# Softmax attention: maxima taken two banks at a time, from four, and no bank kept for transposes

## The chip, the cores and the metric

The kernel runs on one core of one Trainium2 chip. The metric is the device time of the whole program in microseconds (us). Three runs of the kernel before gave 2098.14 to 2100.54 us, median 2099.5.

## The reference

Two transformer-like blocks, each `x = x + attention(layernorm(x)) * silu(ffn(layernorm(x)))`, on `x` of 2 x 2048 x 128 in float32. The first block has linear attention and a top-2 mixture of 8 experts. The second has softmax attention and a top-1 mixture of 8 experts. The change touches only the softmax attention of the second block, cut here to what matters:

```python
b, s, _ = x.shape                       # 2, 2048
q, k, v = (x @ w.T).reshape(b, s, 16, 8)      # 16 heads of 8
q, k = rope(rms_norm(q)), rope(rms_norm(k))
scores = einsum('bqhd,bkhd->bhqk', q / sqrt(8), k)
attn = softmax(scores, axis=-1)         # over 2048 keys
out = einsum('bhqk,bkhd->bqhd', attn, v).reshape(b, s, 128) @ wo.T
```

## The kernel before, in words

The program has stages that follow one another. The first block and the routing, experts and operand preparation of the second fill the first third of the time. Then `softmax_attention` (L1375 to L1692) runs, and `finish` ends the program.

**Chunks.** `softmax_attention` treats two heads of one batch entry at a time (a pair; 16 pairs) and 512 queries at a time (a chunk; 4 per pair, 64 in all). The two heads lie in the two halves of the partitions, 64 rows each. Every chunk has two parts.

**The maxima.** For each block of 128 queries, head and 512 keys, TensorE makes a 128 x 512 tile of scores, queries on the partitions (`for_maxima`, L1507: 32 per chunk), into one of three PSUM banks, in turn. VectorE reduces each to its row maximum (`maxima`, L1659: 32 per chunk), and then all of them to the negated maximum of each query and head (`negate`, L1667). GpSimd splits that into three bf16 parts (`parts`, L1455 to L1465), TensorE transposes them (`shifts`, L1517) into half of bank 7, and ScalarE copies them into rows of the query operand (`take_shifts`, L1623, two copies), so that the next product of keys and queries comes out with the maximum already subtracted.

**The weights.** TensorE makes the scores again, keys on the partitions (`score`, L1524: 32 of 128 x 512 per chunk, three banks in turn). ScalarE takes the exponential (L1630). TensorE multiplies the values by it (`weigh`, L1538: 16 calls per chunk, each four matmuls in the four column tiles of 32, recorded as 8) and accumulates into bank 6; the column tiles are four consecutive `s`, so key tile parity and head, and the two halves of the 512 queries lie in the two halves of the bank. The 33rd value column is ones, so the sum of the exponentials comes out too. At the end of a chunk ScalarE copies the bank (L1648), TensorE transposes the copy and adds the parities (`transposed_sums`, L1582: four matmuls, recorded as 8) into the other half of bank 7, and VectorE takes the reciprocal (L1685) and multiplies (L1690).

**Order.** Each engine's order is written out by hand, and nothing is rearranged at run time. TensorE's main loop makes, at each step `s` of chunk `n`, `score(n, s)` and one maximum of a later chunk: at `s = 8` that is maximum 24 of chunk `n + 1`, so at `s = 16` it goes over to chunk `n + 2`. At every even `s` a `weigh` follows the maximum. After `s = 27` come the shifts of the next chunk, after the last step the transposed sums. A score waits until the exponential has left its bank (three steps earlier); a maximum waits until VectorE has left its bank (three maxima earlier):

```python
pe.wait_ge(m_out, m.at(S, a - earlier(a) + 1 + M_FREE))     # for_maxima
pe.wait_ge(p_ready, n.at(S, s - earlier(s) + 1 + P_FREE))   # score
```

ScalarE's order is the exponentials, with the two shift copies after the 28th and the copy of the sums after the fourth of the next chunk. VectorE's order is the maxima, the negation, and, before maximum 24 of a chunk and after it, the reciprocal and the product of an earlier chunk.

Next to this run SP's loads of the query and key operands of a pair (two pairs ahead) and, during the last two pairs, GpSimd's gathers of the experts' rows.

Of the kernel before, what the change touches and what calls it, by code (L numbers as in the profile page):

```python
# [11 lines left out]
P = 128  # L12
# [40 lines left out]
class Step:  # L53


    def __init__(self, turn, per_turn, number):
        self.turn, self.per_turn, self.number = turn, per_turn, number

    def __add__(self, n):
        return Step(self.turn, self.per_turn, self.number + n)  # L60

    def at(self, each, more):

        constant = self.number * each + more
        return constant if self.turn is None else self.turn * (self.per_turn * each) + constant


# [29 lines left out]
def constants(k, pool):  # L97
# [12 lines left out]
    pool.memset(k.sum_parity[:, :], 0.0).then_inc(cleared, 1)  # L110
# [13 lines left out]
    for group in range(4):  # L124
        head = group % 2
        cols = k.sum_parity[:, 9 * head:9 * head + 9]
# [1238 lines left out]
def softmax_attention(k, U, V, attn, gather):  # L1365
# [7 lines left out]
    UNROLL = 2  # L1373
    S = 2 * NK
    R = 3  # L1375
    PR = 16
    S_BANK, M_BANK, O_BANK, T_BANK = 0, 3, 6, 7
    AHEAD = 24
    SHIFTS_AFTER = 6
    EARLY = 4  # L1380
    NPAIRS = BATCH * PAIRS
    with ExitStack() as ctx:
# [4 lines left out]
        tops = sb("tops", [P, 2, 2 * TPC, QC])  # L1387
# [3 lines left out]
        sumsT = sb("sumsT", [P, CHUNK])  # L1391
        inv = sb("inv", [P, 2 * TPC])
        (cleared, copy_allowed, v_loaded, m_ready, m_out, neg_ready, shift_step, shift_ready, shiftT_ready,
         shift_in, s_ready, p_ready, p_used, sums_out, turned, inv_ready, attn_out) = (
            sem(n) for n in ("cleared", "copy_allowed", "v_loaded", "m_ready", "m_out", "neg_ready",
                             "shift_step", "shift_ready", "shiftT_ready", "shift_in", "s_ready", "p_ready", "p_used",
                             "sums_out", "turned", "inv_ready", "attn_out"))
        q_loaded, k_loaded = k.q_loaded, k.k_loaded
        block = ctx.enter_context(nc.Block())
        GATHERED = TILES // (UNROLL * QC)  # L1400

        M_FREE, P_FREE, U_FREE, O_FREE, T_FREE = R, R, PR // 4, 1, 1
        G = 4

        ahead = Core()
        ahead.turn = None

        def two_on(n):

            return Step(ahead.turn, n.per_turn, n.number + 2 - (0 if n.turn is None else n.per_turn))  # L1410

        def turns(eng, body):
            for pair in range(NPAIRS):
                ahead.turn = None
                body(Step(None, 0, pair), Step(None, 0, pair * QC), pair % 2, pair == NPAIRS - 1)

        @block.sync
        def _(sp):
            for pair in range(2, NPAIRS):

                sp.wait_ge(p_used, (pair - 1) * QC * S // G + U_FREE)
                load_rows(k, sp, U, pair, 0, q_loaded[pair % 2])
                load_rows(k, sp, U, pair, 1, k_loaded[pair % 2])

        @block.gpsimd
        def _(pool):
            pool.memset(shift[:, :, :], 0.0).then_inc(cleared, 1)

            pool.sem_inc(m_out, M_FREE)
            pool.sem_inc(p_ready, P_FREE)  # L1430
            pool.sem_inc(p_used, U_FREE)
            pool.sem_inc(sums_out, O_FREE)
            pool.sem_inc(attn_out, T_FREE)

            def before_copy():

                pool.sem_inc(copy_allowed, 1)

            def load(pair, par):

                before_copy()
                for h in range(2):
                    src = V[:, :, bass.ds(pair.at(2 * DK, h * DK), DK)]
                    nc.gpsimd.tensor_copy(values[par][:, :, h, 0:DK], src).then_inc(v_loaded, 1)

            def parts(m):

                pool.wait_ge(neg_ready, m.at(1, 1))
                if m.turn is not None or m.number > 0:
                    pool.wait_ge(shiftT_ready, m.at(1, 0))  # L1450
                place = lambda i: shift[:, :, :].rearrange("p t (h r) -> p h t r", h=2)[:, :, :, SHIFT + i]
# [3 lines left out]
                nc.gpsimd.tensor_copy(place(0), src).then_inc(shift_step, 1)  # L1455
                pool.wait_ge(shift_step, m.at(4, 1))
                nc.gpsimd.tensor_tensor(rest[0], src, place(0), ALU.subtract).then_inc(shift_step, 1)
                pool.wait_ge(shift_step, m.at(4, 2))
                before_copy()
                nc.gpsimd.tensor_copy(place(1), rest[0]).then_inc(shift_step, 1)  # L1460
                pool.wait_ge(shift_step, m.at(4, 3))
                nc.gpsimd.tensor_tensor(rest[1], rest[0], place(1), ALU.subtract).then_inc(shift_step, 1)
                pool.wait_ge(shift_step, m.at(4, 4))
                before_copy()
                nc.gpsimd.tensor_copy(place(2), rest[1]).then_inc(shift_ready, 1)  # L1465

            pool.wait_ge(cleared, 1)
            for h in range(2):
                nc.gpsimd.tensor_copy(values[0][:, :, h, 0:DK], V[:, :, h * DK:(h + 1) * DK]).then_inc(v_loaded, 1)
            parts(Step(None, 0, 0))  # L1470

            def pair_steps(pair, chunk, par, final):
                for c in range(QC):
                    if not (final and c == QC - 1):
                        parts(chunk + (c + 1))
                    if c == 0 and not final:

                        pool.wait_ge(p_used, pair.at(QC * S // G, U_FREE))
                        load(pair + 1, 1 - par)
                    if pair.number >= NPAIRS - UNROLL:  # L1480
                        first = ((pair.number - (NPAIRS - UNROLL)) * QC + c) * GATHERED
                        for t in range(first, first + GATHERED):
                            gather(pool, t)

            turns(pool, pair_steps)

        half_of = lambda s: s % 2
        other_half_of = lambda a: 1 - a % 2  # L1490
        head_rows = lambda h: slice(h * HEAD_ROWS, (h + 1) * HEAD_ROWS)

        def earlier(s):

            return next(d for d in range(1, 2 * R + 1) if (s - d) % S % R == s % R and (s >= d or (s - d + S) % R == s % R))

        @block.tensor
        def _(pe):
            pe.wait_ge(cleared, 1)

            def for_maxima(m, c, par, a):

                h, qt, kb = other_half_of(a), a // 2 // QC, a // 2 % QC
                rows = head_rows(h)
                pe.wait_ge(m_out, m.at(S, a - earlier(a) + 1 + M_FREE))
                at = (c * TPC + qt) * P
                nc.tensor.matmul(bank[:, M_BANK + a % R, :], queries[par][rows, at:at + P],  # L1507
                                 keys[par][rows, kb * CHUNK:(kb + 1) * CHUNK], start=True, stop=True).then_inc(m_ready, 1)

            def shifts(m):  # L1510

                pe.wait_ge(shift_ready, m.at(1, 1))
                if m.turn is not None or m.number > 1:
                    pe.wait_ge(attn_out, m.at(1, T_FREE - 1))
                out = bank[:, T_BANK, :].bitcast(BF16)
# [4 lines left out]
            def score(n, c, par, s):  # L1520

                pe.wait_ge(p_ready, n.at(S, s - earlier(s) + 1 + P_FREE))
                rows = head_rows(half_of(s))
                nc.tensor.matmul(bank[:, S_BANK + s % R, :], keys[par][rows, (s // 2) * P:(s // 2 + 1) * P],  # L1524
                                 queries[par][rows, c * CHUNK:(c + 1) * CHUNK], start=True, stop=True).then_inc(s_ready, 1)

            def weigh(n, par, g, half):

                if g == 0 and half == 0:
                    pe.wait_ge(sums_out, n.at(1, O_FREE))
                pe.wait_ge(p_ready, n.at(S, 4 * g + 4 + P_FREE))
                at = slice(half * (CHUNK // 2), (half + 1) * (CHUNK // 2))
                for j in range(G):
                    s = G * g + j
                    mm = nc.tensor.matmul(bank[32 * j:32 * j + 32, O_BANK, at], values[par][:, s // 2, s % 2, :],  # L1538
                                          probs[:, s % PR, at], start=(g == 0 and half == 0), stop=(g == S // G - 1 and half == 1),
# [4 lines left out]

            zero = Step(None, 0, 0)
            pe.wait_ge(q_loaded[0], 16 * LOADS[0])
            pe.wait_ge(k_loaded[0], 16 * LOADS[1])
            for a in range(S):
                for_maxima(zero, 0, 0, a)
            for a in range(AHEAD):  # L1550
                for_maxima(zero + 1, 1, 0, a)
                if a == AHEAD // 2:
                    shifts(zero)
            pe.wait_ge(shift_in, 2)
            for s in range(2 * G):
                score(zero, 0, 0, s)
# [399 lines left out]
```

## Time and profile before

| | |
|---|---|
| median of three runs | 2099.5 us (2098.14 to 2100.54) |
| the profiled execution | 2101.37 us, its span 2099.6 us |
| granted TensorE clock, mean of the span | 0.924 of full speed |
| softmax attention | from about 672 us to 2079 us of the span |
| from the first negation of the maxima to the last | 692.1 to 2048.5 us, 63 chunks |

The table's times are those of one execution that was profiled; all durations below come from it. Its own time is 1.9 us above the median of the runs. A start is counted from the beginning of the span. PE is TensorE's matmul, PEld its load of stationary operands, DVE is VectorE, ACT is ScalarE, POOL is GpSimd, SP is SyncE.

### The profile page before, as it was taken

What the parts mean: (1) busy time and instruction counts of PE and PEld (TensorE: products, weight loads), DVE (VectorE), ACT (ScalarE), POOL (GpSimd) and SP (SyncE); (2) the same over time, 40 slices, a digit from 0 to 9 for tenths busy, and PEclk for the clock granted to TensorE, in tenths of its full rate; (3) what the DMA queues carried; (4) which work ended last, traced back from release to release, by engine and by line L of the source; (5) the groups of instructions that cost most, each with busy time, mean ns of one, the idle gap of its engine ahead of it and who ended that gap; (6) DMA issues with size and microseconds to landing.
All of it is one profiled execution on the core that took longest, in us unless ns stands there. A gap on an engine that the chain in (4) does not pass through costs nothing. (4 is left out here: it accounts for less than half of the span.)

```text
span 2099.6 us, 42125 instructions
## 1 busy us (share of the span) xinstructions
PE 1758.9 (84%) x16301; PEld 749.7 (36%) x16301; DVE 1631.6 (78%) x2868; ACT 1462.6 (70%) x2761; POOL 336.0 (16%) x620
## 2 busy tenths in 40 slices
PE   5865879507855999999999999999999999999998
PEld 4544743406832232323333333333333333323334
DVE  3742437624367899999999999999999999999992
ACT  2103546203443588888888888888888888888988
POOL 2371027353032000000000000000000000001211
PEclk9887998558976699999999999999999999999999
DMA  7014111312102001001010010110100101001001
GB/s 243 21 53 114 46 48 52 93 35 70 32 1 32 1 2 17 10 9 17 2 17 14 4 17 2 16 17 1 17 6 13 17 1 17 10 8 22 16 12 51
DMA packets 64253, 61.73 MB, mean 29 GB/s; under 512 B 10720, under 2 KB 52704, under 8 KB 64064
## 3 DMA queue, kind: packets, MB, share of 16 engines
q1 hardware_dynamic: 57920, 46.56, 9.7%
q0 software_dynamic: 6144, 12.60, 2.0%
q8 instruction: 125, 2.05, 0.4%
q14 instruction: 64, 0.52, 0.1%
HBM read 23.21 MB, written 22.94 MB: 22 GB/s over the span
## 5 line engine op out<-in xcount | busy, mean ns | idle before, releaser
L1659 DVE TENSOR_REDUCE at_tops<-bank 128x1 f32<-128x512 f32 x2048 | 1264.1, 683 | 62.4 <-PE bank L1507 43.0
L1630 ACT ACTIVATE at_probs<-bank 128x512 f32<-128x512 f32 x2048 | 1109.6, 598 | 141.3 <-PE bank L1524 114.5
L1507 PE MATMUL bank<-keys,queries 64*128 64x512 bf16 x2048 | 682.0, 390 | 20.8 <-DVE at_tops L1659 19.1
L1524 PE MATMUL bank<-queries,keys 64*128 64x512 bf16 x2048 | 650.5, 383 | 56.2 <-ACT at_probs L1630 56.2
L1538 PE MATMUL bank<-at_probs,values 128*32 128x256 f32 x8192 | 655.5, 392 | 12.2 <-ACT at_sumsT L1648 8.7
L1524 PEld LDWEIGHTS bank<-queries,keys 64*128 64x128 bf16 x2048 | 131.1, 93 | 510.3 <-ACT at_probs L1630 362.8
L1538 PEld LDWEIGHTS bank<-at_probs,values 128*32 128x32 f32 x8192 | 161.8, 108 | 326.8 <-ACT at_probs L1630 191.0
L1455 POOL CAST at_shift<-at_neg 128x8 bf16<-128x8 f32 x64 | 14.0, 219 | 1239.7 <-DVE at_neg L1667 1239.7
L1507 PEld LDWEIGHTS bank<-keys,queries 64*128 64x128 bf16 x2048 | 169.8, 93 | 113.6 <-DVE at_tops L1659 85.2
L669 DVE COPY ep_weights<-WB 128x642 f32 x72 | 35.8, 497 | 91.4 <-DVE ep_slots L680 46.6
L1623 ACT ACTIVATE queries<-bank 3x512 bf16<-3x512 bf16 x128 | 75.4, 589 | 31.4 <-PE bank L1517 28.3
L1096 DVE COPY ffn_w<-W 128x512 f32 x39 | 19.9, 511 | 83.7 <-issue 42.4
L696 ACT ACTIVATE ep_hT<-bank,ep_weights 128x128 f32<-128x128 f32 x144 | 45.1, 365 | 48.8 <-PE bank L638 48.7
L1195 PE MATMUL bank<-wqkv,xnT 128*128 128x384 f32 x64 | 40.0, 801 | 37.6 <-DVE op_qk L1317 32.5
L303 POOL DMA_INDIRECT sorted_pairs<-g_rows,pair_slot x64 | 62.4, 974 | 52.0 <-DVE pair_slot L550 32.8
L1582 PE MATMUL bank<-sum_parity,at_sumsT 128*128 128x18 f32 x512 | 68.2, 267 | 0.8 <-ACT at_sumsT L1648 0.8
L638 PE MATMUL bank<-ep_slotsT,ep_weights 128*128 128x128 f32 x288 | 52.0, 305 | 19.3 <-DVE ep_weights L669 19.3
L1582 PEld LDWEIGHTS bank<-sum_parity,at_sumsT 128*128 128x128 f32 x512 | 61.9, 191 | 15.5 <-issue 15.5
L733 POOL DMA_INDIRECT g_rows<-made_of_pairs,pair_slot x32 | 31.2, 975 | 142.1 <-SPq L714 132.6
L830 DVE RECIPROCAL qg_den<-qg_den 128x512 f32<-128x512 f32 x8 | 26.8, 3353 | 34.0 <-ACT qg_den L799 34.0
L1103 ACT ACTIVATE ffn_slotsT<-bank 128x512 f32<-128x512 f32 (+1 forms) x10 | 5.7, 586 | 67.1 <-PE bank L1039 66.8
L638 PEld LDWEIGHTS bank<-ep_slotsT,ep_weights 128*128 128x128 f32 x288 | 38.7, 196 | 31.2 <-DVE ep_weights L669 29.6
(248 smaller groups left out, 1522.5 us busy)
## 6 DMA issues: line engine op xcount, KB each, us to landing
queries<-query_parts SPq DMA_DIRECT2D x192, 32.0 KB
keys<-key_parts SPq DMA_DIRECT2D x192, 32.0 KB
sorted_pairs<-zeros SPq DMA_DIRECT2D x16, 288.0 KB, 3.7
ep_slots<-sorted_pairs SPq DMA_DIRECT2D x6, 768.0 KB, 9.2
made_of_pairs<-ep_slots SPq DMA_DIRECT2D x6, 768.0 KB, 4.1
sorted_tokens<-zeros SPq DMA_DIRECT2D x8, 312.0 KB, 3.4
ffn_slots<-sorted_tokens SPq DMA_DIRECT2D x3, 832.0 KB, 7.7
made_of_sorted<-ffn_slots SPq DMA_DIRECT2D x3, 832.0 KB, 4.3
```

The source lines that it names most:

```text
L303: pool.indirect_dma_start(sorted_dram, bass.IndirectOffsetOnAxis(ap=r0.slot[i][:, t:t + 1], axis=0), rows[:, t, :], None).then_inc(scatter ...
L638: mm = nc.tensor.matmul(bank[:, H_BANK + u, i * P:(i + 1) * P], wt[:, u, i * P:(i + 1) * P], slotsT[:, j // TPC % TR, j % TPC * P:(j % TPC ...
L669: nc.vector.tensor_copy(wt[:, j % R, :], WB[:, bass.ds(at, STRIDE0)]).then_inc(w_ready, 1)
L696: nc.scalar.activation(hT[:, u, i * P:(i + 1) * P], bank[:, H_BANK + u, i * P:(i + 1) * P], ACT.Relu, bias=wt[:, u, B1_AT + i:B1_AT + i + ...
L1195: mm = nc.tensor.matmul(bank[:, t, 0:3 * D], xnT[:, at:at + P], w.wqkv[:, :], start=True, stop=True)
L1507: nc.tensor.matmul(bank[:, M_BANK + a % R, :], queries[par][rows, at:at + P], keys[par][rows, kb * CHUNK:(kb + 1) * CHUNK], start=True, st ...
L1524: nc.tensor.matmul(bank[:, S_BANK + s % R, :], keys[par][rows, (s // 2) * P:(s // 2 + 1) * P], queries[par][rows, c * CHUNK:(c + 1) * CHUN ...
L1538: mm = nc.tensor.matmul(bank[32 * j:32 * j + 32, O_BANK, at], values[par][:, s // 2, s % 2, :], probs[:, s % PR, at], start=(g == 0 and ha ...
L1582: mm = nc.tensor.matmul(bank[:, T_BANK, 256 + 18 * t:256 + 18 * (t + 1)], sumsT[:, t * P:(t + 1) * P], k.sum_parity[:, :], start=True, sto ...
L1623: nc.scalar.activation(queries[par][rows, c * CHUNK:(c + 1) * CHUNK], bank[rows, T_BANK, 0:CHUNK // 2].bitcast(BF16), ACT.Copy).then_inc(s ...
L1630: nc.scalar.activation(probs[:, s % PR, :], bank[:, S_BANK + s % R, :], ACT.Exp).then_inc(p_ready, 1)
L1659: nc.vector.tensor_reduce(tops[:, m.number % 2, other_half_of(a) * TPC + a // 2 // QC, a // 2 % QC:a // 2 % QC + 1], bank[:, M_BANK + a % ...
```

## The change

Only `softmax_attention` and one constant change.

1. **Two banks per maximum.** The maxima have four banks (3 to 6), as two places of two banks. A unit is two tiles of one head and query block, 1024 keys. VectorE reduces both banks in one instruction of 128 x 1024: 16 per chunk in place of 32. TensorE's first tile of a unit waits until VectorE has left the whole place, two turns earlier (`turn_taken`).
2. **Transposes take turns.** The transposed sums have no bank of their own any more: they take one turn of the maxima's places per chunk (`sums_turn`), after the last unit of a chunk, and VectorE's reciprocal and product, now one behind the other after the negation, end that turn. The shifts take one turn of the scores' three banks, between `s = 27` and `s = 28` (`SHIFT_BANK`), so that score 30 waits for the two shift copies. Scores 28 and 29, and also 31 and 0 to 2 of the next chunk, wait for the exponential two steps earlier in place of three.
3. **Column tiles.** The four column tiles of `weigh` are query halves by heads of one key tile. The accumulator is 256 columns wide in place of 512, the copy of the sums too, and the transposed sums are two matmuls (recorded as 4) against 36 columns in place of four against 18. The order of heads among the scores and maxima changes: two steps of one head, then two of the other, a score and its neighbouring maximum always of different heads.
4. **Order.** The transposed sums of chunk `n - 1` come at `s = 15` of chunk `n`. The first `weigh` of a chunk moves from `s = 6` to `s = 8`, where there are then two in a row. The copy of the sums stands after the fourth exponential as before. The first eight scores are interleaved with the first maxima. The step of the main loop is otherwise the same: score, maximum, and at even `s` a `weigh`; `AHEAD = 24` stays.

Cut to its core (the pool's and SP's code changes in how it is written only; the constant `sum_parity` of 18 columns becomes `sum_columns` of 36):

```diff
+    UNITS = 2 * TPC * 2
+    HALF = CHUNK // 2
+    S_BANK, M_BANK, O_BANK = 0, 3, 7
+    SHIFTS_AT = 28
+    COPY_AT, SUMS_AT = 4, 16
+        head_of = lambda s: s // 2 % 2
+        unit_of = lambda u: (1 - u % 2, u // 4, u // 2 % 2)
+        score_bank = lambda s: S_BANK + (s if s < SHIFTS_AT else s + 1) % R
+        SHIFT_BANK = S_BANK + SHIFTS_AT % R
+        unit_turn = lambda m, u: m * UNITS + u + max(0, m - 2)
+        sums_turn = lambda n: min(n + 3, NCHUNKS) * UNITS + n
+        place = lambda turn: M_BANK + turn % 2 * 2
...
+            def maximum(m, a):
+                u = a // 2
+                h, qt, half = unit_of(u)
+                turn = unit_turn(m, u)
+                if a % 2 == 0 and turn >= 2:
+                    pe.wait_ge(turn_taken, turn - 1)
...
+                mm = nc.tensor.matmul(bank[:, place(turn) + a % 2, :], queries[pair % 2][rows, at:at + P],
+                                      keys[pair % 2][rows, kb * CHUNK:(kb + 1) * CHUNK], start=True, stop=True)
+                if a % 2:
+                    mm.then_inc(m_ready, 1)
...
+            def score(n, s):
+                if s == SHIFTS_AT + R - 1 and n + 1 < NCHUNKS:
+                    pe.wait_ge(shift_in, 2 * (n + 2))
+                else:
+                    before = s - R if s < SHIFTS_AT else s - R + 1
+                    if s < R:
+                        before += 1
+                    if n * S + before >= 0:
+                        pe.wait_ge(p_ready, n * S + before + 1)
...
+            def transposed_sums(n):
+                turn = sums_turn(n)
+                pe.wait_ge(turn_taken, turn - 1)
+                pe.wait_ge(sums_out, n + 1)
...
+            for n in range(NCHUNKS):
+                ahead = (n + 1) * S + AHEAD
+                for s in range(FIRST_SCORES, S if last else S + FIRST_SCORES):
+                    m = n + s // S
+                    score(m, s % S)
+                    if ahead < NCHUNKS * S:
+                        maximum(*divmod(ahead, S))
+                        ahead += 1
+                    if s == SHIFTS_AT - 1 and not last:
+                        shifts(n + 1)
+                    if s == SUMS_AT - 1 and n:
+                        transposed_sums(n - 1)
+                    if s % G in (0, 2):
+                        half = 0 if s % G == 2 else 1
+                        g = s // G - 1 - half
+                        m, g = n + g // (S // G), g % (S // G)
+                        if g or half:
+                            if g == 0:
+                                weigh(m, 0, 0)
+                            weigh(m, g, half)
...
+            def maxima(m):
+                for u in range(UNITS):
+                    h, qt, half = unit_of(u)
+                    at = place(unit_turn(m, u))
+                    dve.wait_ge(m_ready, m * UNITS + u + 1)
+                    nc.vector.tensor_reduce(tops[:, m % 2, h * TPC + qt, half:half + 1], bank[:, at:at + 2, :].rearrange("p b n -> p (b n)"),
+                                            X_AXIS, ALU.max).then_inc(turn_taken, 1)
...
+            for m in range(NCHUNKS):
+                maxima(m)
+                negate(m)
+                if m >= 2:
+                    sums(m - 2)
```

## Rows read from the trace of the kernel before

**Rows 1.** Page, busy time of each engine, its share, instructions

```profile
PE 1758.9 (84%) x16301; PEld 749.7 (36%) x16301; DVE 1631.6 (78%) x2868; ACT 1462.6 (70%) x2761; POOL 336.0 (16%) x620
```

**Rows 2.** Stretches: us, busy us (instructions) by engine, clock, DMA share, GB/s

```profile
672.00:700.00 28.00, 26.67 (x51) 4.80 (x51) 27.16 (x46) 0.53 (x1) 1.72 (x8) 0.50 0.00 1
717.57:2048.50 1330.93, 1246.53 (x12661) 408.46 (x12657) 1252.89 (x2171) 1180.59 (x2172) 95.93 (x364) 1.00 0.07 11
```

**Rows 3.** Groups by line, 717.57 to 2048.50: busy us, mean ns | idle before

```profile
L1659 DVE TENSOR_REDUCE at_tops<-bank 128x1 f32<-128x512 f32 x1984 | 1225.3, 683 | 55.2 <-PE bank L1507 35.8 <-issue 0.4
L1630 ACT ACTIVATE at_probs<-bank 128x512 f32<-128x512 f32 x1986 | 1078.0, 597 | 133.6 <-PE bank L1524 106.9
L1648 ACT ACTIVATE at_sumsT<-bank 128x512 f32<-128x512 f32 x62 | 37.0, 597 | 13.7 <-PE bank L1538 13.7
```

**Rows 4.** Timeline, TensorE, one chunk: start us, us, instruction

```profile
1404.76 0.39 PE L1524 MATMUL bank<-queries,keys 64*128 64x512 bf16 x1
1404.76 0.60 PE L1507 MATMUL bank<-keys,queries 64*128 64x512 bf16 x2
1404.99 0.38 PE L1524 MATMUL bank<-queries,keys 64*128 64x512 bf16 x1
1405.30 0.64 PE L1538 MATMUL bank<-at_probs,values 128*32 128x256 f32 x8
1405.87 0.39 PE L1524 MATMUL bank<-queries,keys 64*128 64x512 bf16 x1
...
1409.55 0.39 PE L1507 MATMUL bank<-keys,queries 64*128 64x512 bf16 x1
1409.87 0.64 PE L1538 MATMUL bank<-at_probs,values 128*32 128x256 f32 x8
1410.44 0.39 PE L1524 MATMUL bank<-queries,keys 64*128 64x512 bf16 x1
...
1410.76 0.40 PE L1517 MATMUL bank<-identb,at_shift 128*128 128x128 bf16 x4
1411.09 0.39 PE L1524 MATMUL bank<-queries,keys 64*128 64x512 bf16 x1
```

**Rows 5.** Timeline, VectorE, the same chunk

```profile
1404.52 0.19 DVE L1667 TENSOR_REDUCE at_neg<-at_tops 128x8 f32<-128x32 f32 x1
1408.82 0.68 DVE L1659 TENSOR_REDUCE at_tops<-bank 128x1 f32<-128x512 f32 x1
1415.78 0.69 DVE L1659 TENSOR_REDUCE at_tops<-bank 128x1 f32<-128x512 f32 x1 [0.21 <-PE bank L1507]
...
1421.28 0.21 DVE L1690 TENSOR_TENSOR xnT<-bank,at_inv 128x64 f32<-128x64 f32 x1
1421.56 4.28 DVE L1659 TENSOR_REDUCE at_tops<-bank 128x1 f32<-128x512 f32 x7
```

**Rows 6.** Timeline, the matmul just before a reduction that waited

```profile
1415.33 0.60 PE L1507 MATMUL bank<-keys,queries 64*128 64x512 bf16 x2
```

**Rows 7.** Groups by line, VectorE, whole span, operands of 1024 elements

```profile
L1317 DVE TENSOR_TENSOR op_qk<-bank,op_st 128x1024 f32<-128x1024 f32 x8 | 9.8, 1224 | 0.3
L1305 DVE TENSOR_REDUCE op_st<-op_squares 128x128 f32<-128x1024 f32 x8 | 9.7, 1218 | 27.8 <-ACT op_squares L1233 27.8
```

**Rows 8.** Timeline, ScalarE, around the shift copies of that chunk

```profile
1405.18 0.60 ACT L1630 ACTIVATE at_probs<-bank 128x512 f32<-128x512 f32 x1 [0.68 <-PE bank L1524]
1405.68 0.59 ACT L1630 ACTIVATE at_probs<-bank 128x512 f32<-128x512 f32 x1
1410.16 1.30 ACT L1630 ACTIVATE at_probs<-bank 128x512 f32<-128x512 f32 x2
1411.48 1.20 ACT L1623 ACTIVATE queries<-bank 3x512 bf16<-3x512 bf16 x2
1412.71 2.73 ACT L1630 ACTIVATE at_probs<-bank 128x512 f32<-128x512 f32 x5
```

**Rows 9.** Timeline, TensorE and VectorE, transposed sums; last the end of the stage

```profile
1418.90 0.39 PE L1507 MATMUL bank<-keys,queries 64*128 64x512 bf16 x1
1419.21 1.07 PE L1582 MATMUL bank<-sum_parity,at_sumsT 128*128 128x18 f32 x8
1420.21 0.39 PE L1524 MATMUL bank<-queries,keys 64*128 64x512 bf16 x1
1420.32 0.21 DVE L1685 RECIPROCAL at_inv<-bank 128x8 f32<-128x8 f32 x1 [0.26 <-PE bank L1582]
2062.59 0.21 DVE L1685 RECIPROCAL at_inv<-bank 128x8 f32<-128x8 f32 x1 [13.91 <-PE bank L1582]
2062.83 0.22 DVE L1690 TENSOR_TENSOR xnT<-bank,at_inv 128x64 f32<-128x64 f32 x1
2074.48 1.83 PE L1538 MATMUL bank<-at_probs,values 128*32 128x256 f32 x24
```

**Rows 10.** Groups by line, ScalarE, a copy of 256 columns from PSUM

```profile
L413 ACT ACTIVATE kr_kvT<-bank 128x256 f32<-128x256 f32 x2 | 0.8, 384 | 17.4 <-PE bank L354 17.4
```

**Rows 11.** Waits, 717.57 to 2048.50: us in total, times, longest us

```profile
PEld bank L1524 <- ACT at_probs L1630: 349.3, 807, 0.7
PEld bank L1507 <- DVE at_tops L1659: 58.0, 173, 0.8
DVE at_tops L1659 <- PE bank L1507: 35.8, 124, 0.4
```

More of the change, by code:

```diff
@@ L50 @@
     pass
[L53 to L65, printed above, removed]
 def bc(ap, shape):
@@ L1470, in _ @@
[L1470 to L1495, printed above, removed]
+            load(0)
+            parts(0)
+            for n in range(NCHUNKS):
+                pair, c = divmod(n, QC)
+                if n + 1 < NCHUNKS:
+                    parts(n + 1)
+                if c == 0 and pair + 1 < NPAIRS:
+                    if pair:
+                        pool.wait_ge(p_used, n * S // G)
+                    load(pair + 1)
+                if pair >= NPAIRS - 2:
+                    first = (n - (NPAIRS - 2) * QC) * GATHERED
+                    for t in range(first, first + GATHERED):
+                        gather(pool, t)
@@ L1518, in shifts @@
                 mm.then_inc(shiftT_ready, 1)
[L1520 to L1527, printed above, removed]
-                if g == 0 and half == 0:
[L1533 to L1539, printed above, removed]
+            def score(n, s):
+                pair, c = divmod(n, QC)
+                if s == SHIFTS_AT + R - 1 and n + 1 < NCHUNKS:
+                    pe.wait_ge(shift_in, 2 * (n + 2))
+                else:
+                    before = s - R if s < SHIFTS_AT else s - R + 1
+                    if n == 0 and s == 0:
+                        pe.wait_ge(shift_in, 2)
+                    if s < R:
+                        before += 1
+                    if n * S + before >= 0:
+                        pe.wait_ge(p_ready, n * S + before + 1)
+                rows = head_rows(head_of(s))
+                at = keys_of(s) * P
+                nc.tensor.matmul(bank[:, score_bank(s), :], keys[pair % 2][rows, at:at + P],
+                                 queries[pair % 2][rows, c * CHUNK:(c + 1) * CHUNK], start=True, stop=True).then_inc(s_ready, 1)
@@ new lines, in weigh @@
+            def weigh(n, g, half):
+                pair, c = divmod(n, QC)
+                if g == 0 and half == 0:
+                    if c == 0:
+                        pe.wait_ge(v_loaded, 2 * (pair + 1))
+                    if n:
+                        pe.wait_ge(sums_out, n)
+                pe.wait_ge(p_ready, n * S + G * g + 3 + half)
+                kt = 2 * g + half
+                for j in range(4):
+                    q, h = divmod(j, 2)
+                    s = G * g + 2 * h + half
+                    mm = nc.tensor.matmul(bank[32 * j:32 * j + 32, O_BANK, 0:HALF], values[pair % 2][:, kt, h, :],
+                                          probs[:, s % PR, q * HALF:(q + 1) * HALF], start=(kt == 0), stop=(kt == NK - 1),
@@ L1615, in _ @@
-            turns(pe, pair_steps)
+                    shifts(0)
+                if a >= AHEAD - FIRST_SCORES:
+                    score(0, a - (AHEAD - FIRST_SCORES))
+            for n in range(NCHUNKS):
+                last = n == NCHUNKS - 1
+                ahead = (n + 1) * S + AHEAD
[17 more added lines that the diff above has]
+                            weigh(m, g, half)
@@ L1652, in _ @@
+            take_shifts(0)
+            for n in range(NCHUNKS):
+                for s in range(S):
+                    exponential(n, s)
+                    if s == COPY_AT - 1 and n:
+                        sums(n - 1)
+                    if s == SHIFTS_AT - 1 and n + 1 < NCHUNKS:
+                        take_shifts(n + 1)
+            sums(n)
         @block.vector
         def _(dve):
-            TAKEN = AHEAD
-            def maxima(m, of):
-                for a in of:
-                    dve.wait_ge(m_ready, m.at(S, a + 1))
-                    nc.vector.tensor_reduce(tops[:, m.number % 2, other_half_of(a) * TPC + a // 2 // QC, a // 2 % QC:a // 2 % QC + 1], bank[:, M_BANK + a % R, :], X_AXIS,
-                                            ALU.max).then_inc(m_out, 1)
```

257 lines of the change are left out of this document (86 added, 171 removed).

## Prediction

> **What bounds the kernel now.** I read the page first: over the whole span no engine is full [rows 1], but that is an average over stages. The stretch between the second and the last negation of the maxima is 62 equal chunks of softmax attention, 1330.93 / 62 = 21.47 us each, at TensorE's full granted clock, the higher of its two levels, 2.4 GHz [rows 2]. There VectorE is busy 94% of the time, TensorE 94% (modelled) and ScalarE 89%. Of VectorE's 20.2 us per chunk, 19.8 are the 32 maxima (1225.3 / 62), and it waits 0.9 us per chunk (55.2 / 62) just before one of them [rows 3]. Seven maxima in a row take 4.28 us [rows 5]: one each (4.28 - 0.68) / 6 = 0.60 us, though each lasts 0.68 until its end is known. So VectorE sets the pace now. The waits say the same: TensorE waits 58.0 us for VectorE to free a bank, in 173 places, VectorE only 35.8 for TensorE [rows 11].
>
> TensorE is close behind. Two steps (two scores, two maxima, one `weigh`) take 1405.87 - 1404.76 = 1.11 us: a score and its maximum run side by side, the next two start 0.23 later, the `weigh` 0.31 after them, and 0.57 after its start comes the next score [rows 4]. Sixteen of these are 17.8 us.
>
> **The two-bank reduction.** No reduction of two banks is in the trace. The nearest rows are a VectorE instruction that reads 1024 elements from two banks, 1.224 us, and a reduction of 1024 elements from SBUF, 1.218 us [rows 7]. Upper bound: two single ones, 2 x 0.68 = 1.36. I take 1.22. Since it is 0.54 longer than a single one, the next can start 0.60 + 0.54 - 0.01 = 1.13 us after it. Against 2 x 0.60 that saves 0.07 per unit, or 1.1 us per chunk, for an engine that is always fed.
>
> **The wait that comes with it.** Will it be fed? There are two places, so the maximum that opens a unit (M0) must wait until the reduction two turns earlier has ended. TensorE keeps its order: at 1409.55 a maximum had waited for the reduction that ran from 1408.82 to 1409.50, and the `weigh` behind it started only at 1409.87, the next score at 1410.44 [rows 4, 5]. In the new order M0 of every unit stands at an even `s`, and the `weigh` is right behind it; the unit's second maximum (M1) comes with the next score. The way round one place is therefore:
> - M0 to the score after the `weigh`, and M1 beside it: 1410.44 - 1409.55 = 0.89 [rows 4];
> - M1 to the start of its reduction: 1415.78 - 1415.33 = 0.45 [rows 5, 6];
> - the reduction until its end: 1.22 [rows 7];
> - end of a reduction to the maximum that waited for it: 1409.55 - 1409.50, 0.06 [rows 4, 5].
>
> That is 2.62 us per place, and with two places one unit every 1.31 us. This is longer than VectorE's 1.13, longer than TensorE's 1.11 and longer than 2 x 0.60 = 1.20 now. Before, three single banks gave 0.68 + 0.06 + 0.45 = 1.19 us of way against 3 x 0.60 = 1.80 of time: 0.6 to spare for a `weigh`. Now there is nothing to spare: the gap from M0 to M1 may be at most 2 x 1.13 - 0.45 - 1.22 - 0.06 = 0.53, and it is 0.89. VectorE will stand still 0.18 us before each unit, and TensorE 0.2 before each M0, with `weigh`, score and M1 queued behind. Sixteen units: 8 x 2.62 = 20.96 us.
>
> **The 17th turn.** The transposed sums take a turn. The next chunk's first unit uses the place of the last unit and follows it at 2.62 as ever; the second one takes the place of the sums, may follow the first at TensorE's pace, and its reduction 1.13 after the first's. VectorE's share (the negation 0.19, from reciprocal to product 2062.83 - 2062.59 = 0.24, from product to the next maximum 1421.56 - 1421.28 = 0.28 [rows 5, 9]) lies inside the way that TensorE needs. So from last unit to last unit: 2.62 + 1.13 + 7 x 2.62 = 22.09 us. The sums' own matmuls are halved (8 took 1.0 us up to the next score [rows 9], 4 about 0.5) and are ready before VectorE comes to them.
>
> **The shifts in the scores' banks.** I follow unit 5 (`s` = 26, 27) with M0 at 0. Score 27 at 0.89, its exponential 0.42 later at 1.31 (1405.18 - 1404.76 [rows 4, 8]). The shifts start 0.32 after score 27, score 28 0.33 later, at 1.54 [rows 4], a little late for its place. The copies start 0.62 after exponential 27 (the second of the two from 1410.16 starts at 1410.86, the copies at 1411.48) and take 1.20 [rows 8]: they end at 3.13. Score 29 at 2.43. Score 30, which could go at 2.65, now waits for the copies: 3.19, and M0 of unit 7 with it, 0.57 behind its place's time. The next exponentials start at 3.15 and 3.65 (they follow at 0.50: 1405.18, 1405.68 [rows 8]); score 31 waits for the second to end at 4.25, in place of 4.08. M1 of unit 7 is at 4.31, its reduction at 4.76 against 2.62 + 0.89 + 0.45 = 3.96: 0.80 us per chunk, on the place that hands over to the next chunk.
>
> **Two `weigh` in a row.** At `s` = 8 the gap from M0 to M1 grows by the second one. Its price isn't in the trace alone: three with their waits took 1.83 against 0.64 for one, so at most 0.60 each [rows 4, 9]; at least nothing. I take 0.5, as it has the passes of the first. The other place then comes 0.89 + 0.5 + 0.22 = 1.6 after it, not 1.2 to 1.3: 0.4 us. The free step at `s` = 6 returns almost nothing, since VectorE's 1.13 holds there.
>
> **The sum.** 22.09 + 0.80 + 0.40 = 23.3 us per chunk, 1.83 more than 21.47. Over 61 of the 62 chunks: +112 us. At the start TensorE runs at half clock with maxima alone (0.50 [rows 2]); 28 units there save 28 x 0.07 = 2 us, and the eight scores moved among them about 1: -3, with -6 to +1 as bounds. The last two chunks have no maxima and stay as they are. 2101.4 (the profiled execution's own time) + 109 = 2210; it stands 1.9 over the median, so **2208 us** is forecast.
>
> **Edits at no cost.** The copy of the sums goes from 0.597 [rows 3] to about 0.384 [rows 10]: ScalarE, 11% idle, gains 0.2 us that nobody waits for. The column tiles of `weigh` keep their number, size and passes. The wider constant is made long before. SP waits for the same count of `weigh` groups, and its loads run two pairs ahead with longer pairs to hide in; GpSimd's parts have 12 steps between the negation and the shifts. If TensorE became the bound, the halved sums would show as -0.5 per chunk.
>
> **A rule weighed against the trace.** VectorE's row in this stage is 94% busy, yet what ends its waits is TensorE [rows 2, 11]. The Trainium skill (Perfetto Trace Analysis, Optimizing Scalar/DVE Operations) has a rule for either case: grouping into larger operations helps where the engine is saturated; where it is not and leaves bubbles on other engines, breaking instructions up lets work be completed sooner. By its first half the time would be that of rival 1, by its second the one I forecast; the trace so far agrees with the first half for three single banks, and no row shows two places.
>
> **Rivals.**
> 1. *VectorE stays fed, and the change is faster* (0.09). If the `weigh` did not stand in the way round a place (gap of M0 to M1 under 0.53), a unit costs 1.13 and a chunk 16 x 1.13 + 0.8 = 18.9; with TensorE's 17.8 + 0.4 + 0.5 beside it, say 19.2: 2099.5 - 61 x 2.27 - 3 = 1958. For it: VectorE's share. Against it: rows that show `weigh` held behind a waiting maximum.
> 2. *Only the way round counts* (0.12): the stops at the shifts and the double `weigh` vanish in slack that I have missed. 22.09 per chunk: 2099.5 + 61 x 0.62 - 3 = 2134.
> 3. *Two banks cost as two instructions* (0.06): the change does not do what it says for VectorE. 1.36 gives (0.89 + 0.45 + 1.36 + 0.06) / 2 = 1.38 a unit, 1.2 more per chunk: 2208 + 61 x 1.2 = 2281. The rows of 1024 speak against it.
>
> My own case has 0.72; in 0.01 gains and stops cancel. Its own range is 2170 to 2245: the reduction between 1.20 and 1.30, the second `weigh` between 0 and 0.6, the stops at the shifts 0.4 less or 0.2 more, the start's bounds. The range of 8 in 10 takes in rival 2: 2130 to 2245. A difference of 0.2%, 4 us, is about what can be told from none: slower 0.90, same 0.01, faster 0.09.
>
> **What would show it.** Right: negations 23.3 us apart; reductions of about 1.22 us that start 1.1 to 1.5 apart, 1.31 on average; idle time of VectorE before most of them, ended by the maxima's matmul, near 0.2 each; a long wait of PEld at the maxima for VectorE in hundreds of places; score 30 of each chunk waiting for the shift copies; VectorE's busy share down from 94% to about 85%. Wrong: if reductions follow one another at 1.13 with no idle time, my way round a place is wrong; if they last 1.36, rival 3; if TensorE's clock in the stage falls from 1.00, every gap on it grows and the time passes 2245.

## The result, and the profile after

The changed kernel takes 2208.4 us (median of four runs, 2206.5 to 2210.3), the kernel before 2100.0 in the same comparison: a ratio of 1.0513, 95% interval 1.0498 to 1.0529. It is slower by 5%; 2208 was forecast. One of the four runs of the single-bank kernel with two repairs (below) took 5250.6 us and the other three 1999.4 to 2001.6, so its median and its ratio are of those three.

The whole difference lies in the softmax stage. From the second negation of the maxima to the last there are again 62 chunks, now in 1441.86 us: 23.26 each against 21.47 [rows 2]. That is 1441.86 - 1330.93 = 110.9 us more. From the first negation to the second it takes 21.3 us in place of 25.5, from the start of the span to the first it takes 2.3 us more, and from the last negation to the end it takes 51.1 us in both kernels. 110.9 - 4.2 + 2.3 = 109.0, which is the difference of the two spans, 2208.6 - 2099.6.

First the page of the kernel after, then the stretch of the 62 chunks and the groups by line in it, as in [rows 1 to 3]:

```profile
PE 1856.8 (84%) x16045; PEld 753.3 (34%) x16045; DVE 1589.5 (72%) x1844; ACT 1448.9 (66%) x2761; POOL 336.3 (15%) x620
```

```profile
715.65:2157.51 1441.86, 1348.38 (x12399) 412.70 (x12396) 1211.44 (x1176) 1166.37 (x2170) 95.89 (x364) 1.00 0.06 10
```

```profile
L1623 DVE TENSOR_REDUCE at_tops<-bank 128x1 f32<-128x1024 f32 x992 | 1180.3, 1221 | 221.7 <-PE bank L1484 220.3
L1598 ACT ACTIVATE at_probs<-bank 128x512 f32<-128x512 f32 x1984 | 1076.3, 598 | 242.0 <-PE bank L1513 229.3
...
L1604 ACT ACTIVATE at_sumsT<-bank 128x256 f32<-128x256 f32 x62 | 23.8, 384 | 30.7 <-PE bank L1529 30.7
```

VectorE does less: 992 reductions of 1.221 us in place of 1984 of 0.683 [rows 3], 1211 us busy in place of 1253 [rows 2]. But it is now busy 84% of the stretch, not 94%, because it stands 221.7 us before the maxima in place of 55.2. ScalarE does the same exponentials and stands 242 us before them in place of 134. No engine is full; TensorE's granted clock is 1.00, its higher level, as before. The waits of the same stretch say who holds whom (the scores, then both directions between VectorE and the maxima, last score 30 behind the shift copies; compare [rows 11]):

```profile
PEld bank L1513 <- ACT at_probs L1598: 450.7, 1037, 0.6
...
DVE at_tops L1623 <- PE bank L1484: 220.3, 557, 0.8
PEld bank L1484 <- DVE at_tops L1623: 156.0, 357, 0.5
PEld bank L1513 <- ACT queries L1590: 40.9, 62, 0.7
```

VectorE waits for TensorE 220 us (35.8 before) and TensorE for VectorE 156 us (58.0 before). Two engines that wait for each other, both with room, point to a way round that is too long. The timeline shows that way, first VectorE, then TensorE:

```profile
1414.00 1.23 DVE L1623 TENSOR_REDUCE at_tops<-bank 128x1 f32<-128x1024 f32 x1 [0.83 <-PE bank L1484]
...
1416.62 1.22 DVE L1623 TENSOR_REDUCE at_tops<-bank 128x1 f32<-128x1024 f32 x1 [0.27 <-PE bank L1484]
```

```profile
1415.28 0.39 PE L1484 MATMUL bank<-keys,queries 64*128 64x512 bf16 x1
1415.60 0.64 PE L1529 MATMUL bank<-at_probs,values 128*32 128x256 f32 x8
1416.17 0.39 PE L1513 MATMUL bank<-queries,keys 64*128 64x512 bf16 x1
1416.17 0.39 PE L1484 MATMUL bank<-keys,queries 64*128 64x512 bf16 x1
```

The reduction from 1414.00 ends at 1415.23; the first maximum of the next unit in its place starts 0.05 later; the `weigh` follows it, and only then, 0.89 after it, the second maximum; the reduction starts 0.45 after that, at 1416.62. From reduction to reduction in one place it takes 2.62 us.

### The profile page after: what moved, and what is told of

Read it like the earlier page. It is cut to its first block and busy times, and to the rows that moved or that the text cites. A ratio compares the mean times of both kernels' runs of the same rounds, so it can differ in the third digit from the quotient of the medians.

```text
span 2208.6 us, 40579 instructions
## 1 busy us (share of the span) xinstructions
PE 1856.8 (84%) x16045; PEld 753.3 (34%) x16045; DVE 1589.5 (72%) x1844; ACT 1448.9 (66%) x2761; POOL 336.3 (15%) x620
## 3 DMA queue, kind: packets, MB, share of 16 engines
HBM read 23.21 MB, written 22.94 MB: 21 GB/s over the span
## 5 line engine op out<-in xcount | busy, mean ns | idle before, releaser
L1623 DVE TENSOR_REDUCE at_tops<-bank 128x1 f32<-128x1024 f32 x1024 | 1217.9, 1221 | 225.9 <-PE bank L1484 224.6
L1484 PE MATMUL bank<-keys,queries 64*128 64x512 bf16 x2048 | 744.2, 392 | 23.0 <-DVE at_tops L1623 16.4
L1513 PE MATMUL bank<-queries,keys 64*128 64x512 bf16 x2048 | 672.8, 384 | 65.5 <-ACT at_probs L1598 28.4
L1529 PE MATMUL bank<-at_probs,values 128*32 128x256 f32 x8192 | 641.1, 390 | 0.0
L1513 PEld LDWEIGHTS bank<-queries,keys 64*128 64x128 bf16 x2048 | 144.4, 93 | 554.3 <-ACT at_probs L1598 462.2
L1484 PEld LDWEIGHTS bank<-keys,queries 64*128 64x128 bf16 x2048 | 177.9, 93 | 230.6 <-DVE at_tops L1623 185.1
L1529 PEld LDWEIGHTS bank<-at_probs,values 128*32 128x32 f32 x8192 | 168.0, 108 | 253.4 <-issue 241.1
L653 DVE COPY ep_weights<-WB 128x642 f32 x72 | 35.8, 497 | 88.6 <-DVE ep_slots L664 46.6
L622 PE MATMUL bank<-ep_slotsT,ep_weights 128*128 128x128 f32 x288 | 51.8, 304 | 19.2 <-DVE ep_weights L653 19.2
L1541 PE MATMUL bank<-sum_columns,at_sumsT 128*128 128x36 f32 x256 | 40.6, 284 | 14.0 <-DVE at_tops L1623 13.4
L1023 PE MATMUL bank<-ident,ffn_slots 128*128 128x128 f32 x39 | 8.3, 374 | 48.4 <-DMA ffn_slots<-sorted_tokens 48.1
```

The costliest lines, as they stand in the source:

```text
L622: mm = nc.tensor.matmul(bank[:, H_BANK + u, i * P:(i + 1) * P], wt[:, u, i * P:(i + 1) * P], slotsT[:, j // TPC % TR, j % TPC * P:(j % TPC ...
L653: nc.vector.tensor_copy(wt[:, j % R, :], WB[:, bass.ds(at, STRIDE0)]).then_inc(w_ready, 1)
L1484: mm = nc.tensor.matmul(bank[:, place(turn) + a % 2, :], queries[pair % 2][rows, at:at + P], keys[pair % 2][rows, kb * CHUNK:(kb + 1) * CH ...
L1513: nc.tensor.matmul(bank[:, score_bank(s), :], keys[pair % 2][rows, at:at + P], queries[pair % 2][rows, c * CHUNK:(c + 1) * CHUNK], start=T ...
L1529: mm = nc.tensor.matmul(bank[32 * j:32 * j + 32, O_BANK, 0:HALF], values[pair % 2][:, kt, h, :], probs[:, s % PR, q * HALF:(q + 1) * HALF] ...
L1541: mm = nc.tensor.matmul(out[:, :, t, :], sumsT[:, n % 2, t * P:(t + 1) * P], k.sum_columns[:, :].rearrange("p (q e) -> p q e", q=2), start ...
```

## The experiments

All times are medians; ratios are to the kernel before in the same comparison. "Per chunk" is the mean time between two negations of the maxima in the profiled execution, first interval left out. Unless said otherwise, an experiment changes the kernel after.

| | median us | ratio (95% interval) | per chunk us |
|---|---|---|---|
| the change | 2208.4 | 1.0513 (1.0498 to 1.0529) | 23.26 |
| weigh at odd steps | 2086.0 | 0.9923 (0.9907 to 0.9940) | 21.24 |
| scores three steps back | 2179.3 | 1.0366 (1.0349 to 1.0384) | 22.79 |
| no two weigh in a row | 2188.4 | 1.0410 (1.0393 to 1.0428) | 22.94 |
| single banks, four of them | 2046.5 | 0.9731 (0.9715 to 0.9748) | 20.65 |
| two banks, the three repairs | 2036.7 | 0.9702 (0.9686 to 0.9718) | 20.49 |
| the same, maxima before score 30 | 2036.8 | 0.9704 (0.9687 to 0.9720) | 20.49 |
| single banks, two repairs | 1999.7 | 0.9528 (0.9509 to 0.9547) | 19.93 |
| the same, maxima before score 30 | 1995.8 | 0.9503 (0.9487 to 0.9518) | 19.85 |
| two banks, later copy of the sums | 2002.1 | 0.9534 (0.9518 to 0.9550) | 19.93 |
| the same, maxima before score 30 | 2001.4 | 0.9533 (0.9517 to 0.9549) | 19.93 |
| the same, transposed sums later | 2011.0 | 0.9583 (0.9567 to 0.9599) | 20.10 |

**The weigh out of the way round.** Only its parity moves, so that the two maxima of a unit stand side by side.

```diff
-                    if s % G in (0, 2):
-                        half = 0 if s % G == 2 else 1
+                    if s % G in (1, 3):
+                        half = 0 if s % G == 3 else 1
```

> The weigh is moved from the even steps to the odd ones, so that the two maxima of a unit stand side by side (0.22 us apart, not 0.89); nothing else changes. Way round a place (mine): (0.22 + 0.45 + 1.22 + 0.06) / 2 = 0.98 us per unit, less than VectorE's 1.13, so VectorE sets the pace between the stops; these stay (shifts in the scores' banks, two weigh in a row) and now hit VectorE directly. About 21.4 us per chunk in place of 23.26, so 2208 - 62 x 1.85 = 2095 us, 2080 to 2110; reductions mostly 1.14 us apart. Rival, the loss comes from the stops and the turns alone, not from the weigh in the way round: unchanged, 2200 to 2215.

The median is 2086 us: 122 us come from these two lines, and the kernel is 0.8% faster than the one before. VectorE's timeline shows seven reductions that are fed without a wait, on average (8.20 - 1.22) / 6 = 1.16 us apart, and three stops in a chunk, of 1.02, 0.66 and 0.16 us:

```profile
1403.26 4.62 DVE L1623 TENSOR_REDUCE at_tops<-bank 128x1 f32<-128x1024 f32 x4 [1.02 <-PE bank L1484]
1408.53 2.35 DVE L1623 TENSOR_REDUCE at_tops<-bank 128x1 f32<-128x1024 f32 x2 [0.66 <-PE bank L1484]
1411.05 3.49 DVE L1623 TENSOR_REDUCE at_tops<-bank 128x1 f32<-128x1024 f32 x3 [0.16 <-PE bank L1484]
...
1415.27 8.20 DVE L1623 TENSOR_REDUCE at_tops<-bank 128x1 f32<-128x1024 f32 x7
```

The rival, that the loss lies in the stops and turns alone, is out.

**The stops one by one.** The scores' waits as the banks need them:

```diff
-                    before = s - R if s < SHIFTS_AT else s - R + 1
+                    before = s - R + 1 if s in (SHIFTS_AT, SHIFTS_AT + 1) else s - R
...
-                    if s < R:
-                        before += 1
```

> Only the distance of the scores' waits changes: scores 31, 0, 1 and 2 wait for the exponential three steps earlier, as their banks need, in place of two. Mine: score 31 no longer waits 0.23 us for exponential 29 behind the shift copies, and score 0 not 0.25 for exponential 30; the place that hands over gains what it lost there, about 0.45 us per chunk: 2208 - 62 x 0.45 = 2180 us, 2170 to 2192. Rival, the stops at the shifts vanish in slack: unchanged, within 5 us of 2208.

And the first weigh of a chunk at its own step:

```diff
+            weigh(0, 0, 0)
             for n in range(NCHUNKS):
...
-                        if g or half:
-                            if g == 0:
-                                weigh(m, 0, 0)
-                            weigh(m, g, half)
+                        weigh(m, g, half)
```

> The first weigh of a chunk goes back to step 6, so that no two stand in a row at step 8; the copy of the sums (0.384 us after the last weigh of the chunk before, two steps earlier) should be done by then. Mine: 0.4 us less per chunk on the place that hands over: 2208 - 62 x 0.4 = 2183 us, 2175 to 2195. Rival 1: the double weigh hides in slack, 2208 within 5. Rival 2: the weigh at step 6 now waits for the copy of the sums and holds TensorE, 2208 to 2230.

The medians are 2179.3 and 2188.4 us. That is 0.47 and 0.32 us less per chunk, both times are inside their ranges, and so neither stop was hidden in slack.

**The reading alone undone.** The same four banks, turns, order and column tiles, but VectorE reads and frees each bank by itself:

```diff
-                if a % 2 == 0 and turn >= 2:
-                    pe.wait_ge(turn_taken, turn - 1)
+                if turn >= 2:
+                    first = taken_before[turn - 2] + 1
+                    pe.wait_ge(turn_taken, first if turn - 2 in sums_turns else first + a % 2)
...
-                    nc.vector.tensor_reduce(tops[:, m % 2, h * TPC + qt, half:half + 1], bank[:, at:at + 2, :].rearrange("p b n -> p (b n)"),
+                    for i in range(2):
+                        dve.wait_ge(m_ready, m * S + 2 * u + i + 1)
+                        kb = half * 2 + i
+                        nc.vector.tensor_reduce(tops[:, m % 2, h * TPC + qt, kb:kb + 1], bank[:, at + i, :],
...
```

> Only the two-bank reading is undone: the same four banks, turns, order and column tiles, but VectorE reduces each bank by itself (32 of 128 x 512 per chunk) and frees it by itself, so a maximum waits four banks back. Mine: the way round a bank is 0.45 + 0.68 + 0.06 and at most 0.66 for a weigh, 1.85 us, against 4 x 0.60 = 2.4 that VectorE needs for four; VectorE sets the pace: 31 x 0.60 + 0.79 + 0.09 + 0.23 + 0.28 = 20.0 us per chunk and part of the stops, 20.0 to 21.0, so 2010 to 2075 us: faster than both kernels although VectorE has more to do. Rival, the turns and the order cost the time and the two-bank reading gains 1.1 us per chunk: 2208 + 62 x 1.1 = 2275 us.

The median is 2046.5 us. With the order as it was changed, the two-bank reading costs 162 us. Everything else in the change, the fourth bank, the turns, the column tiles and the order, gains 55 us together; these four were not measured one by one. VectorE has more to do and is fed: from 900 to 1900 us its 1550 reductions wait 23.7 us for TensorE:

```profile
L1629 DVE TENSOR_REDUCE at_tops<-bank 128x1 f32<-128x512 f32 x1550 | 944.3, 682 | 28.1 <-PE bank L1489 23.7
```

**Both readings with the stops repaired.** Two banks with all three edits above, and single banks with the last two:

> Two-bank reading with the three repairs together: weigh at odd steps, scores waiting three steps back, no two weigh in a row. Mine: from 21.24 us per chunk with the first repair alone, the second takes about 0.45 and the third up to 0.3 (the copy of the sums now follows a weigh one step later and may hold the first weigh of the chunk): 20.5 to 20.9, so 2086 - 62 x 0.55 = 2052 us, 2040 to 2070. VectorE's own 18.9 is not reached, because the scores stop for the shift copies and TensorE needs 17.8 + 0.4 + 0.5 us anyway. Rival, the three stops overlap once VectorE sets the pace, and nothing is left to gain: 2075 to 2090.

> Single-bank reductions with four banks, scores waiting three steps back and no two weigh in a row (weigh at even steps as in the change). Mine: VectorE sets the pace, 20.0 us per chunk; of the 0.65 us that the single-bank run still lost to stops these two repairs return most: 20.0 to 20.3, so 2046 - 62 x 0.5 = 2015 us, 2005 to 2030. Rival, with four banks the stops were hidden already and the 0.65 has another cause: 2040 to 2050.

The medians are 2036.7 and 1999.7 us, both somewhat under their ranges. Single banks come down to what VectorE needs, estimated at 20.0 and measured at 19.93; two banks stay at 20.49, far from VectorE's 18.9. The stretch from 900 to 1900 us of the one with single banks shows VectorE at 99%:

```profile
900.00:1900.00 1000.00, 976.00 (x10034) 288.53 (x10034) 989.90 (x1756) 928.75 (x1756) 74.14 (x290) 1.00 0.08 12
```

Then both with the maxima of steps 30 and 31 before score 30, which waits for the shift copies:

```diff
+                    ready = 2 if s == SHIFTS_AT + 2 else 0 if s == SHIFTS_AT + 3 else 1
+                    early = s == SHIFTS_AT + 2
+                    if not early:
+                        score(m, s % S)
+                    for _ in range(ready):
...
+                    if early:
+                        score(m, s % S)
```

> As the kernel with the three repairs, and at steps 30 and 31 both maxima are issued before score 30, so that the wait for the shift copies no longer holds a unit's maxima; the wait itself stays. Mine: the reduction of that unit is no longer late, but TensorE itself loses the 0.5 us of the stop and is late for the units after it, so little comes of it: 2035 to 2060 us. Rival, VectorE is what the stop hurts, and freeing the maxima gives 0.6 to 0.8 us per chunk back: 2000 to 2015 us.

> As the last one, and at steps 30 and 31 both maxima stand before score 30. Mine: what is left of the stop at the shift copies goes, VectorE is fed all the time, 19.9 to 20.1 us per chunk: 2003 to 2018 us. Rival, TensorE's lost time shows here too: no change against the last one within 4 us.

For two banks nothing changes, as expected. Single banks gain 4 us, which is just what the rival allowed, and give the fastest kernel of all, 1995.8 us: 5.0% faster than the kernel before and under the range that was given. In the same stretch its reductions never wait for TensorE.

**Where the two-bank kernel's rest goes.** With the weigh at odd steps the last one of a chunk comes a step later, and ScalarE stood before the copy of the sums, 41.1 us in 49 chunks of the two-bank kernel with three repairs:

```profile
ACT at_sumsT L1600 <- PE bank L1527: 41.1, 49, 0.8
```

The next kernel has the weigh at odd steps, scores three steps back, the two weigh in a row, and the copy two exponentials later:

```diff
-    COPY_AT, SUMS_AT = 4, 16
+    COPY_AT, SUMS_AT = 6, 16
```

> Two-bank reading, weigh at odd steps, scores three steps back, the two weigh in a row at step 9 as the change has them, and the copy of the sums after the sixth exponential in place of the fourth. In the kernel with the three repairs VectorE stood still three times a chunk: about 0.2 and 0.63 us at the shift copies, 0.74 us at the copy of the sums, which held ScalarE until the last weigh of the chunk before, now a step later, was done. Mine: the third stop goes and the double weigh brings about 0.3 back: 20.49 - 0.45 = 20.0 us per chunk, 2036.7 - 62 x 0.45 = 2009 us, 1998 to 2022. Rival, TensorE sets that kernel's pace and the stop at the copy is hidden: 2032 to 2045.

The median is 2002.1 us, inside its range, and this wait is no longer among those of the kernel. Then the maxima before score 30 again:

> As the last one, and at steps 30 and 31 both maxima stand before score 30. Mine: with the stop at the copy of the sums gone TensorE can make good what it loses at the shift copies, so freeing the maxima there now shows: 0.3 to 0.6 us per chunk, 1970 to 1992 us, below the best single-bank kernel (1996). Rival, as in the pair before, TensorE's own loss is what counts: no change against the last one within 4 us.

The median is 2001.4 us. That is the rival's outcome, and my theory missed. The last one puts scores 16 and 17 ahead of the transposed sums and the two maxima behind them:

> As the last one, and scores 16 and 17 are issued before the transposed sums and the two maxima that follow them (in the last kernel TensorE stands about 0.76 + 0.26 us per chunk before the transposed sums, waiting for VectorE to leave their place, with everything else queued behind). Mine: TensorE sets the pace there, its own work is 17.8 + 0.4 + 0.6 + 0.4 = 19.2 us and the rest up to 19.92 is this wait; two scores in front fill about 0.45 of it: 19.5 us per chunk, 2001 - 62 x 0.45 = 1973 us, 1968 to 1985, faster than the best single-bank kernel (1996). Rival, the wait is hidden behind VectorE's own pace: 1997 to 2005.

The median is 2011.0 us: slower, and again a miss. The timelines of TensorE in the last two kernels say why. First without the edit, then with it:

```profile
1407.42 0.39 PE L1511 MATMUL bank<-queries,keys 64*128 64x512 bf16 x1
...
1407.65 0.38 PE L1484 MATMUL bank<-keys,queries 64*128 64x512 bf16 x1
1408.29 0.64 PE L1539 MATMUL bank<-sum_columns,at_sumsT 128*128 128x36 f32 x4 [0.26 <-DVE at_tops L1627]
1408.85 0.64 PE L1527 MATMUL bank<-at_probs,values 128*32 128x256 f32 x8
1409.42 0.39 PE L1511 MATMUL bank<-queries,keys 64*128 64x512 bf16 x1
```

```profile
1413.49 0.60 PE L1511 MATMUL bank<-queries,keys 64*128 64x512 bf16 x2
1414.02 0.63 PE L1539 MATMUL bank<-sum_columns,at_sumsT 128*128 128x36 f32 x4
1414.59 0.60 PE L1484 MATMUL bank<-keys,queries 64*128 64x512 bf16 x2
1415.12 0.64 PE L1527 MATMUL bank<-at_probs,values 128*32 128x256 f32 x8
1415.69 0.39 PE L1511 MATMUL bank<-queries,keys 64*128 64x512 bf16 x1
```

Without the edit the sums start 0.64 after the last maximum, where 0.31 is the usual distance [rows 9]: they lose 0.33, not the 0.76 + 0.26 of idle time that I had read as a wait. The block takes 1409.42 - 1407.42 = 2.00 us. With the edit nothing waits, but two scores run without maxima beside them and two maxima without scores, and the block takes 1415.69 - 1413.49 = 2.20. The difference, 0.20, is close to the chunk's, 0.17 (20.10 against 19.93). So TensorE's own work is on the path there, and taking a score and its maximum apart costs more (0.53) than the wait that went (0.33). The same pairing is broken where both maxima stand before score 30; that this is what cancels the gain there was not measured by itself.

The best kernels of the two readings, 2001.4 and 1995.8 us, are only 6 us apart. The 162 us are thus what the two-bank reading costs in the order of the change; most of them went when calls were moved.

## Why the prediction was right

- **What bounds the kernel.** Before, it is VectorE, with stops: VectorE's work is nearly the same in the fastest single-bank kernel, which needs 19.85 us per chunk where the kernel before took 21.47, so some 1.6 us of each chunk were not VectorE's work. After, it is the way round a place. The distances 0.89, 0.45, 1.22 and 0.05 are in the rows above, and their sum is 2.62 as forecast. The experiment with the weigh at odd steps shows that the first of them decides: with 0.22 in its place the units between the stops follow at the pace of VectorE.
- **The two-bank reduction** takes 1.221 us (forecast 1.22), and a fed one starts 1.13 to 1.14 after the one before. Rival 3 (two banks cost two instructions) falls.
- **The 17th turn** fits in as worked out. The transposed sums start 0.60 us after the last maximum, where 0.31 is the usual distance, so they wait about 0.3 us for their place. The next unit's first maximum then still has to wait for VectorE, so VectorE loses nothing by it: from the last unit's reduction to the next chunk's first it is 2.62 us in most chunks, as forecast.

```profile
1410.84 0.39 PE L1484 MATMUL bank<-keys,queries 64*128 64x512 bf16 x1
1411.44 0.64 PE L1541 MATMUL bank<-sum_columns,at_sumsT 128*128 128x36 f32 x4 [0.22 <-DVE at_tops L1623]
...
1412.66 0.37 PE L1484 MATMUL bank<-keys,queries 64*128 64x512 bf16 x1 [0.27 <-DVE at_tops L1623]
```

- **The stop at the shifts** was put at 0.80. Unit 5's reduction starts at 1420.39 and that of unit 7 at 1423.80, 3.41 apart, 0.79 more than 2.62:

```profile
1420.39 1.21 DVE L1623 TENSOR_REDUCE at_tops<-bank 128x1 f32<-128x1024 f32 x1
...
1423.80 1.23 DVE L1623 TENSOR_REDUCE at_tops<-bank 128x1 f32<-128x1024 f32 x1 [0.65 <-PE bank L1484]
```

- Score 30 waits for the copies in every chunk, and score 31 for an exponential that its bank does not need:

```profile
1422.23 0.39 PE L1513 MATMUL bank<-queries,keys 64*128 64x512 bf16 x1 [0.37 <-ACT queries L1590]
...
1423.34 0.39 PE L1513 MATMUL bank<-queries,keys 64*128 64x512 bf16 x1 [0.15 <-ACT at_probs L1598]
```

- **Two weigh in a row.** The second one costs 0.44 us (16 passes from 1406.07 to the next score at 1407.08, 1.01 against 0.57; the first row below), 0.5 was taken; splitting them returns 0.32, 0.40 was forecast.

```profile
1406.07 1.07 PE L1529 MATMUL bank<-at_probs,values 128*32 128x256 f32 x16
1407.08 0.39 PE L1513 MATMUL bank<-queries,keys 64*128 64x512 bf16 x1
```

- **The sum.** 23.3 us per chunk were forecast, and 23.26 measured. At the start 3 us back were forecast; 4.2 came back between the first two negations, but 2.3 were lost before the first, which leaves 1.9. The chunks were put at 112 us more and gave 110.9. That these two errors of about 1 us cancel is luck; the mechanism and each larger term were right.
- **What was said less well.** I expected VectorE to stand about 0.2 us before most units. It stands before 557 of 992, 0.40 us each (220.3 / 557): the two places do not share the time evenly, and in a pair of units one follows at 1.14 without a wait and the other at 1.49. The mean is the same.
- **Rival 1** (VectorE stays fed, 1958 us) is what happens in the stretches between the stops once the weigh is moved, but its time was not reached: the best two-bank kernel takes 2001. Its sum for TensorE gives 17.8 + 0.4 + 0.5 = 18.7 us, and 19.2 was taken without a row for the rest; that kernel needs 19.93.
- **Rival 2** (the stops vanish in slack, 2134 us) falls, since removing each of two stops gave time back, 0.47 and 0.32 us per chunk.
- **The rule on grouping.** The Trainium skill (Perfetto Trace Analysis, Optimizing Scalar/DVE Operations) has a second half to its rule: where an engine is not saturated but causes bubbles on others, breaking instructions up may let work be completed sooner. This case agrees: in the kernel after, VectorE is 84% busy, TensorE's maxima wait 156.0 us for it in place of 58.0, and single banks from the same four banks were faster by 162 us. By the first half of the Trainium skill's rule VectorE, 94% busy before, looked saturated enough for grouping to pay. Grouping did save it 41 us of work in the stretch, and the kernel became slower.

## What to carry to other kernels

Before enlarging an instruction that frees a buffer, add up the way round the buffer (first write, what stands in the writer's order until the last write, the reader's start, the reader, the release) and divide it by the number of buffers: that, not the reader's busy time, is the pace if it is the larger. Four banks as two places of two gave a way of 2.62 us for two units where four single ones had room; moving one call out of the way (2086 us) or going back to single banks (2046.5 us) was each enough to make it faster than the kernel before. TensorE took its calls in the order in which they are written: the `weigh` started only 0.32 us after the maximum that had waited. So the position of an unrelated call was part of that way.

## What was not expected of the hardware

- Nearly all of the schedule could be added up from five distances of the trace to some hundredths of a microsecond per step: with no change of the granted clock (1.00 in the stretch of the chunks), 60 of the 62 chunks of the kernel after took 23.25 to 23.33 us. The first took 22.12, as it has no transposed sums, and one took 23.42.
- Idle time of the weight-load engine before an instruction (37.9 us in 50 chunks at the transposed sums, 0.76 each, in the last kernel but one) was mostly the usual distance to the instruction before; the loss was 0.33:

```profile
PEld bank L1539 <- DVE at_tops L1627: 37.9, 50, 0.8
```

- Two matmuls on different halves of the rows start 0.003 us or so apart and share 0.22 us, as before; two after one another on the same half need 0.22 each. Splitting two such pairs cost 0.53 us per block in the last experiment; 0.33 of that was saved by the wait that went, and 0.20 remained.
